# Pages of its own for the last batch, and the expert groups of the others moved up behind layer 0

## The reference

```python
xn = _layernorm(x)
s = _L0_attn_ref(xn, ...)            # causal linear attention with rope
g = _silu(_L0_ffn_ref(xn, ...))      # dense MoE: 8 experts of 352, top 2
x = x + s * g
xn = _layernorm(x)
s = _L1_attn_ref(xn, ...)            # attention over the heads of one token, rms, GELU
g = _silu(_L1_ffn_ref(xn, ...))      # MoE: 160 experts of 64, top 8, and a shared expert
x = x + s * g
```

## Time and profile before

| | |
|---|---|
| median of 3 runs | 1617.26 us (1605.86 to 1618.96) |
| profiled execution | 1617.64 us, span 1615.5 us, mean granted clock 0.875 |
| PE, DVE, ACT, POOL busy | 1270.6, 889.2, 553.5, 553.7 us |
| layer 0 (0 to 968 us) | batch after batch |
| between the layers | 968 to 1057 us |
| slots 0 to 49 | 1057 to 1167 us |
| periods and end | 1167 to 1615 us |

### The profile page before, as it was taken

How to read it: one execution, slowest core, us unless ns; L and a number is a source line. 1 busy time by engine, 2 the same in 40 slices (tenths; PEclk the granted TensorE clock), 3 DMA queues, 4 the chain that set the end, 5 groups by cost and what they waited for, 6 DMA issues and landing times. The chain is left out here.

```text
span 1615.5 us, 20441 instructions
## 1 busy us (share of the span) xinstructions
PE 1270.6 (79%) x6336; PEld 704.5 (44%) x6336; DVE 889.2 (55%) x2575; ACT 553.5 (34%) x1170; POOL 553.7 (34%) x574
## 2 busy tenths in 40 slices
PE   3699988988888898889799891179978777877762
PEld 2334333333333333333333331056966656776652
DVE  3345575675665664665765757600054685486561
ACT  1232322322312322312322220157856355545620
POOL 0000043042052052052061162600065666656565
PEclk9589998998998987998999995579989988898975
DMA  8920020210210210210210213168744444444331
GB/s 270 338 98 1 25 80 27 69 41 22 79 36 17 79 36 17 79 34 18 72 41 12 79 46 119 46 219 255 223 134 121 131 137 131 136 132 138 97 90 42
DMA packets 123235, 152.07 MB, mean 94 GB/s; under 512 B 15277, under 2 KB 82413, under 8 KB 122374
## 3 DMA queue, kind: packets, MB, share of 16 engines
q1 hardware_dynamic: 106758, 117.36, 22.5%
q0 software_dynamic: 16384, 33.59, 7.4%
HBM read 73.30 MB, written 77.60 MB: 93 GB/s over the span
## 5 line engine op out<-in xcount | busy, mean ns | idle before, releaser
L1097 POOL DMA_INDIRECT y<-y_rows,idxy x256 | 269.5, 1053 | 283.7 <-DMA y_rows<-ys 136.8
L1064 POOL DMA_INDIRECT rows<-xn,idx x256 | 252.1, 985 | 83.9 <-issue 82.2
L935 ACT ACTIVATE hs<-GY 128x512 f32<-128x512 f32 x176 | 105.3, 598 | 377.6 <-PE GY L695 306.6
L711 PE MATMUL ACC<-hs,wff 128*128 128x512 f32 x352 | 200.7, 661 | 0.0
L695 PE MATMUL GY<-xn0T,wff 128*128 128x512 f32 x352 | 189.2, 620 | 0.0
L1038 POOL TENSOR_TENSOR rs<-rs,neg_half 128x4 f32<-128x4 f32 x16 | 16.4, 1024 | 453.1 <-DVE rs L1135 453.1
L701 PE MATMUL B<-xw,wff 128*128 128x512 f32 (+2 forms) x272 | 122.6, 630 | 40.9 <-DVE hs L1428 40.9
L1500 DVE SCALAR_TENSOR_TENSOR pos<-neg,pos 128x1024 f32<-128x1024 f32 x8 | 9.8, 1231 | 262.3 <-issue 192.3
L1428 DVE TENSOR_TENSOR hs<-hs,B 128x512 f32<-128x512 f32 x96 | 65.8, 686 | 128.6 <-PE B L701 65.7
L1242 DVE TENSOR_TENSOR att<-X,causal 128x512 f32<-128x512 f32 x128 | 82.6, 686 | 87.7 <-PE X L583 50.7
L842 PE MATMUL X<-y,ident 128*128 128x128 f32 x480 | 78.0, 329 | 64.1 <-DVE y L1587 60.5
(11 more groups left out here) (274 smaller groups left out, 2180.7 us busy)
## 6 DMA issues: line engine op xcount, KB each, us to landing
xg<-rows SPq DMA_DIRECT2D x104, 256.0 KB
y_rows<-ys SPq DMA_DIRECT2D x104, 256.0 KB
rows<-zero SPq DMA_DIRECT2D x7, 2048.0 KB, 9.5
rows<-zero SPq DMA_DIRECT2D x1, 12288.0 KB, 53.9
wff<-in_wgz SPq DMA_DIRECT2D x2, 3840.0 KB, 38.4
wd<-in_wd SPq DMA_DIRECT2D x1, 5120.0 KB, 24.8
wff<-in_w SPq DMA_DIRECT2D x3, 1408.0 KB, 9.2
rows<-xn,idx POOLq DMA_INDIRECT x256
```

Source lines behind the costliest of these rows:

```text
L711: nc.tensor.matmul(ACC[:, :], w2_0[:, v, :], hs[:, v % RH, :], start=(v == 0), stop=(v == U0 - 1))\
L935: nc.scalar.activation(hs[:, u % RH, :], G[u % 2][:, :], ACT.Silu).then_inc(sem["silu_ready"], 1)
L1064: pool.indirect_dma_start(rows, bass.IndirectOffsetOnAxis(ap=idx[:, t * 8 + k:t * 8 + k + 1], axis=0), xn1[:, t, :], None)\
L1097: pool.indirect_dma_start(y8[:, i % RG, k, :], None, y_d[0:groups * Q * P, :], bass.IndirectOffsetOnAxis(ap=idxy[:, b, t * 8 + k:t * 8 + k ...
```

## The change

Batch 7 no longer shares pages with the others. It gets 32 extra pages (384 to 415) and 160 fixed ones (416 to 575), so there are 576 pages and 144 groups instead of 104. Batches 0 to 6 need nothing of batch 7 for their groups. The order of groups becomes a list, `ORDER`: 0 to 47; then for each of 7 periods the 8 extra groups as before and behind them 6, 6, 6, 6, 6, 5, 5 of the 40 fixed groups of batch 7 (`BESIDE`). A period is now 14 slots long (13 for the last two before batch 7's), where it was 8. The weighings stand at slots base + 5, 8, 11 and 13, where they stood at + 5, 7, 9 and 10. The gather of batch b waits for `FOR_GATHER[b]` groups, which leaves out the fixed groups behind; batch 7's waits for all 144.

Slot 0 starts right behind layer 0's last unit. What batch 7 needs of layer 0 goes into the slots by the table `SEAM` (PE and ACT), on DVE and POOL it runs beside them. `restart` sets the page counters anew for batch 7. SP waits for the scatters of batches 0 to 6 only, loads rows 0 and 1, then the second half of the gate weights in two quarters (`wg2` needed from group 20, `wg3` from group 30), then goes on with the rows; it stores x1 and xn1T of batch 7 in slots 5 and 9, writes the table in slot 33 and reads it back in slot 35. From the first group of batch 7 on (`FIRST_LAST`, index 56) it waits for batch 7's scatter. The attention of batch 0 stands in slots 37 to 40. The clear for batch 7 is 192 pages (12 MB) instead of 32. PSUM banks and the places of buffers in SBUF are dealt out anew, so that layer-0 steps and groups don't share them.

```diff
-NJ = E1 + NB * MORE_PAGES
+LAST_DYNAMIC = E1 + (NB - 1) * MORE_PAGES
+LAST_STATIC = LAST_DYNAMIC + MORE_PAGES
+NJ = LAST_STATIC + E1
...
-PERIOD0 = GATHER0 + 2
-LAST_SLOT = PERIOD0 + GSTEP * NB + 4
+BESIDE = (6, 6, 6, 6, 6, 5, 5)
+ORDER, FOR_GATHER, BASE = list(range(GATHER0)), [GATHER0], [GATHER0 + 2]
+for b in range(NB - 1):
+    ORDER += range(GATHER0 + GSTEP * b, GATHER0 + GSTEP * (b + 1))
+    FOR_GATHER.append(len(ORDER))
+    first = LAST_STATIC // Q + sum(BESIDE[:b])
+    ORDER += range(first, first + BESIDE[b])
+    BASE.append(len(ORDER) + 2)
+FOR_GATHER[NB - 1] = len(ORDER)
+PERIOD0, PERIOD7 = BASE[0], BASE[NB - 1]
+LAST_SLOT = PERIOD7 + GSTEP + 4
+FIXED = [g < SG or g >= LAST_STATIC // Q for g in ORDER]
...
+FIRST_LAST = min(FIRST_LAST, ORDER.index(LAST_STATIC // Q))
+SEAM = {1: ["res_T"], 6: ["xn1_T"], 7: ["xn1T_copy"], 9: ["router1"], 10: ["probs1"], 15: ["rank"]}
+STORE_X1, STORE_XN1, TABLE_OUT, TABLE_IN = 5, 9, 33, 35
...
-front(0, -5)
-plan(-1, ("mix", 0, 0), ("mix", 0, 2), ("rms", 0, 0))
...
+front(0, 37)
+plan(40, ("mix", 0, 0), ("mix", 0, 2), ("rms", 0, 0))
+tail(0, PERIOD0 + 3)
 for b in range(NB):
-    base = PERIOD0 + GSTEP * b
+    base = BASE[b]
     more = b + LEAD < NB
+    w = (5, 8, 11, 13) if more else (5, 7, 9, 10)
...
-    plan(base + 5, ("weigh", b, 0))
+    plan(base + w[0], ("weigh", b, 0))
...
-        tail(b + LEAD, base + 11 if b + LEAD + 1 < NB else base + 10)
-    plan(base + 9, ("weigh", b, 2))
-    plan(base + 10, ("weigh", b, 3), ("end", b, 0))
+        tail(b + LEAD, BASE[b + 1] + 3 if b + LEAD + 1 < NB else BASE[b + 1] + 2)
+    plan(base + w[2], ("weigh", b, 2))
+    plan(base + w[3], ("weigh", b, 3), ("end", b, 0))
...
                 if units and "res" in want:
-                    clear(rows, (b - 1) * MORE_PAGES + FIRST_PAGES, MORE_PAGES, "zeros")
+                    if isinstance(b, int) and b == NB - 1:
+                        clear(rows, LAST_DYNAMIC, NJ - LAST_DYNAMIC, "zeros7")
+                    else:
+                        clear(rows, (b - 1) * MORE_PAGES + FIRST_PAGES, MORE_PAGES, "zeros")
...
+            def load_rows(k):
+                if k == FIRST_LAST:
+                    sp.wait_ge(sem["scattered"], 16 * T * TOPK1 * NB)
+                    sp.wait_ge(loaded["zeros7"], 16)
+                if k >= RX:
+                    sp.wait_ge(two["xt_ps"], k - RX + 1)
+                sp.dma_start(xg[:, k % RX, :, :], rows_v[ORDER[k]]).then_inc(two[f"xg{k % RX}"], 16)
...
+                if s == TABLE_IN:
+                    sp.wait_ge(once["tab_out"], 16)
+                    sp.dma_start(tabs[:], tab_d.unsqueeze(0)).then_inc(loaded["tab"], 16)
...
+            sp.wait_ge(sem["scattered"], 16 * T * TOPK1 * (NB - 1))
+            sp.wait_ge(loaded["zeros"], 16 * (NB - 1))
+            sp.wait_ge(sem["s_rot_ready"], NB)
             load_rows(0)
             load_rows(1)
+            sp.wait_ge(sem["acc_done"], NB)
+            for name, i in (("wg2", 2), ("wg3", 3)):
+                sp.dma_start(wgz[:, GZ * i // 4:GZ * (i + 1) // 4], a["wgz"][:, GZ * i // 4:GZ * (i + 1) // 4]).then_inc(loaded[name], 16)
             for s in range(LAST_SLOT):
                 if s + 2 < NG:
                     load_rows(s + 2)
                 if 0 <= s - 4 < NG:
                     store_y(s - 4)
+                seam(s)
...
             for b in range(NB):
-                groups = GATHER0 + GSTEP * b
+                groups = GATHER0 + GSTEP * b if b < NB - 1 else NG
                 for r in range(RY):
-                    pool.wait_ge(two[f"yst{r}"], 16 * len(range(r, groups, RY)))
+                    pool.wait_ge(two[f"yst{r}"], 16 * len(range(r, FOR_GATHER[b], RY)))
```

More of the change, by code:

```diff
@@ L741, in turn, with gate @@
+            def turn(k):
+                pe.wait_ge(two[f"xg{k % RX}"], 16 * (k // RX + 1))
+                if k:
+                    pe.wait_ge(two["xt_ready"], k)
                 for q in range(Q):
-                    last = nc.tensor.transpose(XT[:, q * P:(q + 1) * P], xg[:, n % RX, q, :], ident[:])
+                    last = nc.tensor.transpose(XT[:, q * P:(q + 1) * P], xg[:, k % RX, q, :], ident[:])
                 last.then_inc(two["xt_ps"], 1)
-            def gate(n):
-                if n == SG:
+            def gate(k):
+                if k == SG:
@@ L851, in _ @@
                     gate(s - 1)
-                if 0 <= s - 2 < SG:
+                if 0 <= s - 2 < NG and not FIXED[s - 2]:
+                    turn_h(s - 2)
+                if 0 <= s - 3 < NG and not FIXED[s - 3]:
+                    down(s - 3)
+                if 0 <= s - 2 < NG and FIXED[s - 2]:
                     down_first(s - 2)
-                if SG <= s - 2 < NG:
-                    turn_h(s - 2)
-                if SG <= s - 3 < NG:
-                    down(s - 3)
+                for name in SEAM.get(s, []):
+                    if name in steps:
+                        steps[name](0)
                 for name, b, t in AFTER.get(s, []):
@@ L1016, in _ @@
             steps2 = {n[2:]: f for n, f in locals().items() if n.startswith("d_")}
-            for s in range(min(AFTER), LAST_SLOT):
-                if 0 <= s < NG:
+            steps["res_silu"](0)
+            for s in range(LAST_SLOT):
+                if s < NG:
                     copy_x(s)
@@ L1307, in s_topk1b, with restart @@
                 link(nc.vector.tensor_scalar(s8[:], s8[:], 2.5, None, ALU.mult))
+            def restart():
+                join()
+                for v, x in ((run, 1.0), (pages, 1.0), (given, float(LAST_DYNAMIC))):
+                    link(nc.vector.memset(v[:], x))
+                link(nc.vector.tensor_tensor_scan(shift[:], ones1[:], ones1[:], LAST_STATIC - 1.0, ALU.mult, ALU.add))
+                join()
             def s_place_a(t):
@@ L1467, in _ @@
             layer0(seen, dve.Fori, f0)
+            batch[0] = NB - 1
+            for u in range(4 * U0):
+                for name, t in beside(STEPS, u, {"res"}):
+                    if name == "place_a":
+                        restart()
+                    if name in steps:
+                        steps[name](t)
             join()
```

230 lines of the change are left out of this document (115 added, 115 removed).

## The result

The changed kernel took **1718.85 us** (median of 4 runs, 1716.90 to 1728.97) against 1614.04 of the kernel before (4 runs, 1605.86 to 1618.96): a ratio of **1.071, 95% interval 1.066 to 1.076**. I had forecast 1616, with 1578 to 1648 as the range: wrong, by 103 us.

The account below looks back on a forecast made before the run. Bounds: a nearly empty core between layers, PE in the groups, then periods of 35.3 us DVE followed by 21.2 of PE and ACT. Terms -61.0 + 51.6 + 7.5 = -1.9 took 1617.64 to 1616 us, range 1578 to 1648.

Parts of the forecast that it names:

- The gap closes: Between the layers: slot 0 starts after the scatter of batches 0 to 6, at 971.6 instead of 1056.78, -85.2 us.
- Gate weights ahead of rows 2: Ahead of slot 2: rows 2 wait behind the second half of the gate weights, +8.2 us.
- Router steps, table, front: In the slots before the periods: router steps +5, the table's round trip +5, batch 0's qkv and exp +4 us.
- scatter beside groups: Before the periods: batch 7's scatter runs beside groups that move 512 KB in 1.82 us, +2 us (0 to 6).
- 40 more groups: In the periods: groups behind weigh 2 add 8.9 us each period, making 64.8; +51.6 us over six.
- Rival (a): In the periods: PE's idle time hides the groups wholly or half, 0 to 5 us a period, 1588 us; chance 0.31.
- The end: After the last period: batch 7's gather waits for every group and starts later, +7.5 us.
- (b): At weigh 2: PE's clock falls during the new wait, 4.8 us a period, 29 in all, 1645 us; chance 0.18.
- (c): At index 56: batch 7's scatter is not there in time; at 20 us beyond, 1636 us; chance 0.04.
- (d): Between the layers: groups do not start early, as the clear or batch 6's scatter is late; above 1650 us; chance 0.03.

Follow-up runs that it names:

- the control: The changed kernel itself, nothing altered, timed again in another group of runs against the kernel before: 1517.50 us, a ratio of 0.984.

## Why the prediction was wrong

**The gap closes (-85.2).** Right: -89.1 (967.68 against 1056.78), and -80.3 without pauses. The 4 us are less than what layer 0 differs from trace to trace with pauses.

**Gate weights ahead of rows 2 (+8.2).** Right: 7.34 us of idle ahead of slot 2, ended by the landing of rows, and slot 2 stands 12.4 us behind slot 0, as summed. Rows waited for the weights ahead of them, as the earlier trace rows had said.

**Router steps, table, front (+5, +5, +4) and scatter beside groups (+2).** From slot 0 to the first block I had 24 us more than before, with the weights. It was 28.9 without pauses (149.51 against 120.66), and 48.1 with them. The run without the scatter got 23 of them back (its seam is 155.6): "+2 (0 to 6)" was the first mis-sized term. I had priced the scatter by its bytes; the run with 64-byte rows, which cost the same 35 us, says that bytes were not the price.

**40 more groups (+51.6, a period of 64.8). This is the step that failed:** a period of 78.4, +135.4 for the six. Behind weigh 2 I had taken 21.2 us from before and added 8.9 of work. The work was right. Rival (a) had said in passing that 4.9 of the 21.2 are pauses; without them 16.3 + 8.9 = 25.2 and a period of 60.5, and the control, without pauses, has 59.4. What was wrong is that I carried those 4.9 us of pauses over as they were, and they grew. PE's steps behind weigh 2 in the control, and the same steps in the profiled run with the result:

```profile
1214.03 2.05 PE L883 MATMUL V<-y,ident 128*128 128x128 f32 x16 [0.25 <-DVE y L1650]
1219.81 2.05 PE L883 MATMUL V<-y,ident 128*128 128x128 f32 x16
1223.47 0.81 PE L841 MATMUL X<-wqkv,xin 128*128 128x384 f32 x2
1226.78 0.81 PE L841 MATMUL X<-wqkv,xin 128*128 128x384 f32 x2
1230.08 0.81 PE L841 MATMUL X<-wqkv,xin 128*128 128x384 f32 x2
1233.83 0.81 PE L841 MATMUL X<-wqkv,xin 128*128 128x384 f32 x2
```

```profile
1268.50 3.64 PE L883 MATMUL V<-y,ident 128*128 128x128 f32 x16
1275.86 2.05 PE L883 MATMUL V<-y,ident 128*128 128x128 f32 x16
1283.19 1.73 PE L841 MATMUL X<-wqkv,xin 128*128 128x384 f32 x2 [0.26 <-issue]
1289.98 0.81 PE L841 MATMUL X<-wqkv,xin 128*128 128x384 f32 x2
1293.29 0.81 PE L841 MATMUL X<-wqkv,xin 128*128 128x384 f32 x2
1300.09 0.81 PE L841 MATMUL X<-wqkv,xin 128*128 128x384 f32 x2
```

Weigh 2 to the fourth qkv: 19.8 us and 31.6. The order is the same; the steps behind weigh 2 are those that I listed. This period is 79.7 us, and that of the control 59.4. The 20.3 between them are 3.8 from L1563 to weigh 2 (39.1 against 35.3), 11.8 from there to the fourth qkv, and 4.7 from that to the next L1563 (9.1 against 4.3). What I left out is that POOL's gather now lies beside this chain: it begins 28 us behind L1563, when the store that SP issues in slot base + 9 has landed, and runs nearly to the period's end, 8 of its 32 calls just ahead of weigh 2 and 24 behind it. Before, 19 of the 33 calls between 1243 and 1299.5 lay ahead of weigh 2, in DVE's block, and 14 behind. There a pause of ACT cost nothing: from L1500 to weigh 2 the paused kernel before took 35.3 us, as did the control. I had written that POOL's gather "no longer sets anything": that looked at what waits for POOL, not at what runs beside it.

**The end (+7.5).** Measured +4.9 with pauses, and +0.1 without. The term was too large, but it matters little in the sum.

**Why before didn't show it.** Its period is 55.9 with pauses and 56.3 without. With them PE's and ACT's part behind DVE's block sets it. Without them POOL's chain does, and DVE waits for the gather ahead of weigh 3, 44 us behind the block at 1159.41 (the run with memsets):

```profile
1203.22 1.23 DVE L1594 TENSOR_TENSOR y<-y,w8all 128x1024 f32<-128x1024 f32 x1 [8.59 <-DMA y<-y_rows,idxy]
```

The two bounds happen to be of one length, so the period gave no hint that pauses stood in it. Layer 0 is slower with the condition too: the same code reached its first transpose of pages at 1056.78 and at 983.50.

By condition, changed less before: slot 0 -89.1 or -80.3, seam +48.1 or +28.9, six periods +135.4 or +23.8, end +4.9 or +0.1; sums +99.3 and -27.5. Of the 127 us between them the periods hold 112.

**The rivals.** (a), some of the groups hidden, has the number of what happened where there are no pauses: +4 us a period, and 28 us gained in all where I had forecast 2. Its mechanism is right only in half. The pauses do not stand behind weigh 2 there, but in the kernel before a wait for POOL's gather stands in their place. That rival (a) came near is in part luck. (b), the clock at weigh 2, is seen (3.64 in place of 2.05 at 1268.50) but it follows the pauses: the control, with the same order, has 2.05. The mean granted clock was 0.879 with pauses and 0.924 without; behind weigh 2 (to the next L1563) 0.87 and 1.00. The Trainium skill (TensorE: Matmul & The Clock Gate, HAM oscillation) describes short bursts of matmuls between waits that start slow each time. That fits the slow rows beside the pauses, so it names a part of the loss, but not its source. (c) and (d) did not occur.

**What stays open.** What makes the condition (three of the six groups had it, three not, and one chip had both); by what way POOL's calls reach ACT and PE; whether calls, rows or POOL's time on them set the price; and whether other work of POOL would do the same, since the run with memsets fell into a group without pauses. Refills of instructions are not it: from 1035 to 1080, with some 15 pauses of ACT, the instruction queues moved three packets. The Trainium skill (Runtime: NRT & Kernel Launch, Instruction fetch mechanics) calls their cost mostly hidden, and nothing in this stretch speaks against it.

## What to carry to other kernels

Price a moved step also by what it now runs beside. With the condition, 32 indirect calls of POOL cost up to 35 us beside a chain in which ACT and PE hand to each other every 0.6 us, and nothing measurable beside DVE's block. Where the chain names "issue" or "remote" while inputs are ready, that time is neither work nor slack; take it out of the sum and ask where it will be afterwards. And a verdict of some per cent from one group of runs can turn round in another: time a change in more than one, and put the changed kernel itself into each group of experiments.

## What the runs showed of the hardware

- In three of the six groups of runs, indirect calls of POOL held up ACT, and PE behind it, mostly for 1 to 5 us at a time: 24 to 35 us for 32 calls, with 512 or 64 bytes a row; 32 plain transfers of the same bytes, issued by POOL on the same queue, cost 6.5 and made no pause. DVE isn't seen to be touched: its first and second product for the weighings stand 10.6 us apart beside calls (1255.71 and 1266.35 in the kernel before, with pauses) and without any (1276.66 and 1287.27 in the second run without gathers). The Trainium skill (SBUF — State Buffer, SBUF: two separate sides) says of the engines' ports to SBUF that PE and ACT never wait on anyone, and that a DMA is not slowed by computing, nor the other way round. Whether the pauses are waits at a port no run here shows; if the page holds, they are something else.
- The condition is worth 3 to 5% in the kernel before, which nobody changed (1541 to 1546 us without pauses, 1591 to 1614 with), and 13% in the changed one (1517.50 and 1718.85).
